# A graph network on one core: zero-fill copies cut into rows, and the matrix build in another order

## The chip, the cores and the metric

The kernel runs on one core of one Trainium2 chip. The metric is the device time of one execution in microseconds. Several executions were timed; one more was taken with the hardware profiler, and all rows shown below come from that one.

## What is computed

A graph of 1250 nodes, 512 features each, and 20000 edges sorted by target. Four layers follow each other, each added to its input and normalised:

```python
edge_index = jnp.stack([src, dst])
x = _layernorm(x + _L0_gnn_ref(x, edge_index, edge_weight, ...))      # weighted sum over edges
x = _layernorm(x + _L1_gnn_ref(x, edge_index, edge_type_2, ...))      # two relational layers, weights mixed from 30 bases
x = _layernorm(x + _L2_gnn_ref(x, edge_index, L2_gnn_W, L2_gnn_b))    # degree-normalised sum
x = _layernorm(x + _L3_gnn_ref(x, edge_index, edge_attr_8, ...))      # attention over edges with a bias for each edge
```

## The kernel before

Instead of gathering rows for each edge, the kernel turns the edge list into dense node-by-node matrices once and multiplies with them. Node counts are padded to 1280 (`NN`), ten tiles of 128 rows (`NT`). Five engines have programs of their own, written out by hand in the order in which they run; they meet only at semaphores.

**The build.** Edges lie in 160 chunks of 125. Because they are sorted by target, the edges of 32 target rows (a window) lie in a short range of chunks. There are 40 windows (`TT`), run as ten turns (`t4`) of four (`j`). For each window VectorE makes one-hot selections of the source node, 125 x 1250 in f16, one a chunk (lines 926 and 934), and TensorE multiplies each with the chunk's own values into three PSUM banks (line 1727, three matmuls a visit); windows alternate between two sets of three banks. Four visits (`FIXED`) are written out; the chunks beyond them, at least one a window, are visited in a loop over registers. The selections of the four lie in two sets of four buffers, those of the loop in a ring of `MORE` = 2. Each engine reads the chunk range of the next window from a table in SBUF into registers (`load_range`, lines 463 to 469). The order of a window before the change: on VectorE the first selection, the loop, the read of the range, selections two to four; on TensorE the first visit, the loop, one matmul of the second visit, the correction, the rest of the second visit, the third, the read of the range, the fourth.

ACT copies a finished window from PSUM to `stage16` in f16 (line 1398, `copied`). The correction `fix` on TensorE (line 1711) subtracts this f16 copy in the banks, so that what is left there is its error; ACT evicts that as the low half (line 1400, `evicted`), which frees the banks. SyncE stores the three parts of a window from `stage16` into the matrices `A16` and `CT` (lines 627 and 629, `R<-R`, three transfers of 80 KB); ACT waits for them (`stored`) before it writes the same of the four `stage16` slots again.

**The zero fill.** The attention's edge bias is a node-by-node table of 52 MB in DRAM (`bias_d`), which must be zero before GpSimd adds the edges into it by 160 indirect scatters (line 812). It is cut into 40 cells of 1.31 MB. The first is filled from SBUF; the others are DRAM-to-DRAM copies of it (line 779), all issued by GpSimd on the software queue: two at once, 24 during the build, one each time some windows are built (`built`), one after output tiles 8 and 9 of the first layer each (`o_done`), and eleven after the first relational layer's weights (`w_in`) and the edge data (`b_in`) have landed.

**After the build** come the ten output tiles of the first layer, with the mixing of the relational layer's weights between their matmuls. ACT and VectorE write the mixed weights out in two halves to DRAM (`w_d`, ACT's queue, 32 KB transfers, line 1351), and SyncE loads them back as `W<-w_d` (line 636) before TensorE's first z tile (line 1802), which waits for all four loads.

Of the kernel before, what the change touches and what calls it, by code (L numbers as in the profile page):

```python
# [6 lines left out]
F16 = mybir.dt.float16  # L7
# [8 lines left out]
NT = -(-NODES // P)  # L16
NN = NT * P
# [16 lines left out]
PIECES = [(0, 512), (512, 1024), (1024, NN)]  # L34
HOTS = 8
FIXED = 4
MORE = 2
BIG = 1e30
QUADS = 2
RB = 256  # L40
# [20 lines left out]
def gnn_resnorm(nc, a, out):  # L61
    ctx = ExitStack()
    with ctx:
# [47 lines left out]
        def in_w(n):  # L111
            nonlocal o
            o += n
            assert o <= 3 * FT * D
            return w_b[:, o - n:o]
# [3 lines left out]
        iota16 = in_w(NN // 2).bitcast(F16)  # L119
        tab = in_w(TT + 2)[0:1, :].bitcast(I32)  # L120
        fix16 = in_w(P // 2).bitcast(F16)
        zero = r3[:, NT * D + 2 * NN + CH:NT * D + 3 * NN + CH]
        more = zero.bitcast(F16).rearrange("p (s r) -> p s r", s=MORE)
        key = r3[:, NT * D + 2 * NN:NT * D + 2 * NN + CH]

        o = 0

        def tmp(n):
# [33 lines left out]
        lowrow = tmp(1)  # L162
        minus16 = tmp(P // 2).bitcast(F16)
        assert o <= 6 * NN // 2 + NN // 4
        o = NT * D + 3 * NN + CH
        SUPS = [[w_b[:, k * D // 2:(k + 1) * D // 2].bitcast(F16) for k in range(NT)],
                [w_b[:, (NT + k) * D // 2:(NT + k + 1) * D // 2].bitcast(F16) for k in range(6)] +
                [r3[:, o + k * D // 2:o + (k + 1) * D // 2].bitcast(F16) for k in range(4)]]
        assert o + 4 * D // 2 <= RELS * FT * NN
        wst_first = r1f[:, NT * NN // 2 - 4 * D:NT * NN // 2].bitcast(F16).rearrange(  # L170
            "p (g h q n) -> p g h q n", g=2, q=2, h=2)
        XTP = r3[:, 0:NT * D].rearrange("p (k f n) -> p k f n", k=NT, f=FT)
# [575 lines left out]
        def _(pool):  # L748
# [22 lines left out]
            def zeros(n):  # L771

                cells = bias_d[0:DUMP, :].rearrange("(n p s) h -> n p (s h)", n=ZF, p=P)
                if n < ZS:
                    pool.dma_start(cells[n].rearrange("p (a b) -> p a b", b=NN),
                                   zero.rearrange("p (u n) -> p u n", u=1).broadcast_to([P, 2, NN])).then_inc(
                                       zero_out, 16)
                else:
                    pool.dma_start(cells[n], cells[0]).then_inc(zero_out, 16)  # L779

            for i in range(2):
# [38 lines left out]
        def _(dve):  # L821
# [99 lines left out]
            def make(t4, j):  # L921

                lo, begin, end = range_of(dve, ranges[j % 2])

                def fixed(m):
                    V.tensor_scalar(hot[0:EC, FIXED * (j % 2) + m, 0:NODES], iota16[0:EC, 0:NODES], base[0:EC, bass.ds(t4, 1), j],  # L926
                                    key[0:EC, bass.ds(lo + m, 1)], ALU.add, ALU.is_equal).then_inc(hot_made, 1)

                dve.wait_ge(built, t4 * 4 + (j + 1))
                fixed(0)  # L930
                with dve.Fori(begin, end) as c:
                    v = dve.snap(visited, min_val=0, max_val=TT * CH)
                    dve.wait_ge(more_used, v + 1)
                    V.tensor_scalar(flat(more[0:EC, bass.ds(v & (MORE - 1), 1), 0:NODES]), iota16[0:EC, 0:NODES],
                                    base[0:EC, bass.ds(t4, 1), j], key[0:EC, bass.ds(c, 1)], ALU.add,
                                    ALU.is_equal).then_inc(more_made, 1)
                    dve.reg_add(visited, visited, 1)
                load_range(dve, ranges[(j + 1) % 2], t4 * 4 + (j + 1))
                for m in range(1, FIXED):
                    fixed(m)  # L940

            def windows(t4):
                for j in range(4):
# [11 lines left out]
            with dve.Fori(1, NT) as t4:  # L955
# [6 lines left out]
            V.tensor_copy(SUP[:, 1, 0:6, :].rearrange("p k f -> p (k f)"),  # L962
                          w_b[:, NT * D // 2:(NT + 6) * D // 2].bitcast(F16))
            V.tensor_copy(SUP[:, 1, 6:NT, :].rearrange("p k f -> p (k f)"),
                          r3[:, NT * D + 3 * NN + CH:NT * D + 3 * NN + CH + 4 * D // 2].bitcast(F16)).then_inc(sup_kept, 1)

            def turned_low(n, i):

# [354 lines left out]
        def _(act):  # L1323
# [84 lines left out]
            def mixed_high(m):  # L1408

                g, h = m // 2, m % 2  # L1410
                if h == 0 and m % MIXES >= 4:
                    act.wait_ge(w_stored, 64 * (g - 1))
                act.wait_ge(w_done, m + 1)
                S.activation(WST(m)[:, h, 0, :], mm_out(MIXED(m), D), ACT.Copy).then_inc(wh_made, 1)
                if h == 0 and m % MIXES and m != M0:
                    mix_stored(g - 1)
# [222 lines left out]
        def _(pe):  # L1639
# [80 lines left out]
            def build(j, t4, first):  # L1720
# [11 lines left out]
                def fixed(m, pieces=range(3)):  # L1732
                    if pieces[0] == 0:
                        pe.wait_ge(hot_made, t4 * 16 + (FIXED * j + m + 1))
                    return visit(lo + m, lambda p0, p1: hot[0:EC, FIXED * (j % 2) + m, p0:p1], m == 0, pieces)

                pe.wait_ge(evicted, t4 * 4 + (j + 1))
                fixed(0)
                with pe.Fori(begin, end) as c:
                    v = pe.snap(visited, min_val=0, max_val=TT * CH)  # L1740
                    pe.wait_ge(more_made, v + 1)
                    visit(c, lambda p0, p1: flat(more[0:EC, bass.ds(v & (MORE - 1), 1), p0:p1]),
                          False).then_inc(more_used, 1)
                    pe.reg_add(visited, visited, 1)
                fixed(1, range(1))
                if j:
                    fix(t4, j - 1)
                elif not first:
                    fix(t4 - 1, 3)
                fixed(1, range(1, 3))  # L1750
                fixed(2)
                load_range(pe, ranges[(j + 1) % 2], t4 * 4 + (j + 1))
                for m in range(3, FIXED):
                    ins = fixed(m)
                ins.then_inc(built, 1)

            pe.wait_ge(own_made, 1)
            pe.wait_ge(fix_made, 1)
# [473 lines left out]
```

## Time and profile before

| what | value |
|---|---|
| median of 3 runs | 1253.46 us |
| lowest and highest | 1247.01 and 1256.37 us |
| profiled execution | 1259.67 us |
| its span, first to last instruction | 1257.9 us |
| mean granted TensorE clock in it | 0.982 of full |

The profiled execution is 6.2 us longer than the median; 1.8 us of it lie around the span. Times in rows count from the span's start. Engines are PE (TensorE, PEld its weight loads), DVE (VectorE), ACT, POOL (GpSimd) and SP (SyncE); a q behind a name is the engine's sequencer or DMA queue. `R<-W,R` means that a tile R is written from tiles W and R.

### The profile page before, as it was taken

Reading aid. Unit: us, or ns where it says so; the run is one execution under the profiler, and the core shown is the slowest. Engines: PE = TensorE matmul, PEld = TensorE weight load, DVE = VectorE, ACT = ScalarE, POOL = GpSimd, SP = SyncE. Lnnn points to the kernel's source line nnn. Section 1 sums busy time; section 2 is a strip of 40 time slices with the busy share of each in tenths; the row PEclk is TensorE's granted clock in tenths of the full one; section 3 lists DMA queues with packets and bytes.
Section 4 is the critical chain, followed back from the end, with each engine's and each line's share of the span. In section 5 each row is a group of like instructions: output and inputs, shape, how many; then the busy total and the mean of one; then the engine's idle time right before and its main releaser. Section 6 shows DMA issues by size and latency. Waiting matters only on the chain.

```text
span 1257.9 us, 21464 instructions
## 1 busy us (share of the span) xinstructions
PE 1181.3 (94%) x8083; PEld 540.5 (43%) x8084; DVE 851.3 (68%) x1330; ACT 437.1 (35%) x586; POOL 307.6 (24%) x220
## 2 busy tenths in 40 slices
PE   6987879999999999999999999999999899999997
PEld 2333334323344334345445454455333365555553
DVE  7575657544434555553368875575999889899997
ACT  2444546512122222112311002216553255444454
POOL 2000000000010133344655655545556000000000
PEclk9988989999999999999999999999999899999999
DMA  8567867598799789753122213112223376565653
GB/s 327 209 217 247 297 224 269 151 407 305 243 363 307 257 285 314 278 165 109 2 35 35 50 19 69 2 3 33 34 33 67 139 235 231 202 220 187 213 186 112
DMA packets 64325, 222.73 MB, mean 177 GB/s; under 512 B 31138, under 2 KB 36002, under 8 KB 48272
## 3 DMA queue, kind: packets, MB, share of 16 engines
q1 hardware_dynamic: 34706, 156.38, 35.8%
q0 software_dynamic: 25184, 53.10, 16.7%
q10 hardware_dynamic: 4350, 12.07, 2.8%
q8 instruction: 60, 0.98, 0.3%
q14 instruction: 25, 0.20, 0.0%
HBM read 198.92 MB, written 59.92 MB: 206 GB/s over the span
## 4 chain that ended last, share of the span: by engine, by line
PE 69%; DVE 11%; issue 7%; DMA 7%; ACT 3%; SPq 2%; DVEq 1%; ACTq 0%
PE PS L1853 26%; PE PS L1802 10%; PE PS L1727 6%; PE PS L1657 5%; PE PS L2098 4%; PE PS L2085 4%; DMA R<-R 4%; DVE R L1172 4%; DVE R L1209 4%; PE PS L1675 3%; PE PS L1967 2%; PE PS L2144 2%; PE PS L1889 1%; PE PS L1773 1%; DMA W<-in_basis_s 1%
## 5 line engine op out<-in xcount | busy, mean ns | idle before, releaser
L812 POOL DMA_INDIRECT bias_d<-R x160 | 271.0, 1694 | 331.3 <-DMA bias_d<-R 220.5
L1853 PE MATMUL PS<-R 128*128 128x512 f16 x1300 | 298.1, 381 | 0.0
L1853 PEld LDWEIGHTS PS<-R 128*128 128x128 f16 x1300 | 120.5, 98 | 180.6 <-issue 49.7
L1727 PE MATMUL PS<-R,XX 125*128 125x512 f16 (+2 forms) x612 | 134.7, 354 | 15.3 <-ACT R L1400 6.8
L1613 ACT ACTIVATE R<-PS 128x1024 f32<-128x1024 f32 (+1 forms) x100 | 106.2, 1087 | 109.6 <-PE PS L2085 77.9
L1802 PE MATMUL PS<-W,XX 128*128 128x512 f16 x600 | 136.0, 386 | 5.1 <-DVE R L1010 2.7
L926 DVE TENSOR_SCALAR R<-W,R 125x1250 f16<-125x1250 f16 x160 | 89.4, 606 | 53.7 <-PE PS L1727 39.4
L1172 DVE CUSTOM_DVE_ANT_0 R<-PS,R 128x1250 f16<-128x1250 f32 x80 | 116.8, 1459 | 5.5 <-PE PS L2021 2.9
L2098 PE MATMUL PS<-R 128*32 128x256 f32 (+1 forms) x1600 | 102.5, 391 | 5.2 <-DVE R L1209 5.2
L2085 PE MATMUL PS<-R 128*128 128x256 f16 (+3 forms) x800 | 99.6, 275 | 5.4 <-ACT R L1613 2.2
L779 POOL DMA_DIRECT2D bias_d<-bias_d x39 | 21.6, 556 | 324.0 <-PE PS L1727 164.2
L1010 DVE SCALAR_TENSOR_TENSOR R<-PS,gate,R 128x512 f16<-128x512 f32 x50 | 37.4, 750 | 90.2 <-ACT R L1451 90.2
L1209 DVE SCALAR_TENSOR_TENSOR R<-R,W 128x512 f32<-128x512 f32 (+1 forms) x136 | 86.0, 673 | 15.9 <-ACT R L1613 14.1
L1727 PEld LDWEIGHTS PS<-R,XX 125*128 x612 | 58.3, 100 | 88.6 <-issue 57.5
L1802 PEld LDWEIGHTS PS<-W,XX 128*128 128x128 f16 x600 | 58.1, 99 | 76.9 <-issue 10.3
L2085 PEld LDWEIGHTS PS<-R 128*128 128x128 f16 (+1 forms) x800 | 74.7, 99 | 36.9 <-issue 20.6
L1434 ACT ACTIVATE stat<-stat 128x1 f32<-128x1 f32 x30 | 8.8, 294 | 184.1 <-DVE stat L998 171.7
L1451 ACT ACTIVATE R<-PS,gate 128x512 f16<-128x512 f32 x50 | 34.4, 687 | 98.1 <-PE PS L1802 97.4
L1400 ACT ACTIVATE R<-PS 32x1280 f32 x40 | 49.2, 1230 | 51.8 <-PE PS L1711 51.8
L2098 PEld LDWEIGHTS PS<-R 128*32 128x32 f32 x1600 | 44.8, 109 | 48.7 <-DVE R L1209 13.5
L1967 PE MATMUL PS<-XX,W 128*128 128x512 f16 (+1 forms) x288 | 61.3, 345 | 1.1 <-ACT R L1552 1.1
L970 DVE TENSOR_TENSOR XX<-PS,XX 128x512 f16<-128x512 f32 x40 | 27.5, 686 | 49.3 <-ACT XX L1405 46.7
(231 smaller groups left out, 1411.0 us busy)
## 6 DMA issues: line engine op xcount, KB each, us to landing
bias_d<-bias_d POOLq DMA_DIRECT2D x39, 1280.0 KB, 9.0
R<-in_basis_s SPq DMA_DIRECT2D x32, 1024.0 KB, 6.9
W<-in_basis_s SPq DMA_DIRECT2D x28, 1024.0 KB, 6.1
W<-bias_d SPq DMA_DIRECT2D x27, 1024.0 KB, 4.9
XX<-bias_d SPq DMA_DIRECT2D x13, 1024.0 KB, 4.9
R<-key_d SPq DMA_DIRECT2D x20, 500.0 KB, 4.0
R<-R SPq DMA_DIRECT2D x120, 80.0 KB, 5.9
W<-bias_d SPq DMA_DIRECT2D x7, 904.0 KB, 4.6
```

The costliest lines, as they stand in the source:

```text
L812: pool.indirect_dma_start(bias_d, bass.IndirectOffsetOnAxis(ap=idx[:, c:c + 1], axis=0), attr[:, c, :], None, bounds_check=DUMP + GC * P - ...
L926: V.tensor_scalar(hot[0:EC, FIXED * (j % 2) + m, 0:NODES], iota16[0:EC, 0:NODES], base[0:EC, bass.ds(t4, 1), j], key[0:EC, bass.ds(lo + m, ...
L1172: V.tensor_tensor_reduce(out=junk[:, 0:NODES], in0=PS[:, b0:b0 + 3, :].rearrange("p a b -> p (a b)")[:, 0:NODES], in1=nmask[:, i, 0:NODES] ...
L1209: ins = V.scalar_tensor_tensor(p, p, BIG, b, ALU.min, ALU.mult)
L1613: S.activation(ER[n % 4][:, :, 0:w, :].rearrange("p g r u -> p g u r"), PS[:, 2 * (n % 2):2 * (n % 2) + 2, :].rearrange("p a (e r) -> p a ...
L1657: ins = T.matmul(PS[32 * c:32 * c + RELS * FT, MIXED(m), :], attbd[0:BJ, layer, :, :].rearrange("p r j -> p (r j)"), BASIS(m)[0:BJ, c, :], ...
L1727: ins = T.matmul(mm_out(3 * (j % 2) + b, p1 - p0), own[0:EC, bass.ds(c, 1), :, :].rearrange("p c m w -> p (c m w)"), hots(p0, p1), start=f ...
L1802: ins = T.matmul(mm_out(zi % 2, D), lhs, rhs, start=n == 0, stop=n == len(terms) - 1)
L1853: ins = T.matmul(mm_out(SUM_BANK(s, i), D), lhs, rhs, start=n == 0, stop=n == len(terms) - 1)
L1967: ins = T.matmul(mm_out(BANK_OF("q", g), hi - lo), W16[:, 1 + which, q, f, o_ * P:(o_ + 1) * P], XT16[:, p, f, lo:hi], start=n == 0 and f ...
L2085: ins = T.matmul(PS[:, 2 * (n % 2) + i // 2, (i % 2) * RB:(i % 2) * RB + w], key[:, h, j * P:(j + 1) * P], query[:, h, cols], start=k == 0 ...
L2098: ins = T.matmul(PS[32 * i:32 * i + 32, 4 + q, e * RB:e * RB + w], VA[:, j, 4 * q + i, 32 * e:32 * e + 32], ER[n % 4][:, i // 2, 0:w, i % ...
```

## The change

Three things change together. The 39 copies of the zero fill take the 128 rows of 10 KB of a cell as even rows and then odd rows, on both sides, instead of as one piece. The order of a window changes: on VectorE three selections, the loop, the read of the range, the fourth selection; on TensorE two visits, the correction, the third visit, the loop, the read of the range, the fourth visit. And the loop's ring has four slots instead of two; to make room, `key` and four tiles of the first layer's support move to another tile (`W`), where the mixed weights will be staged, so ACT waits for `sup_kept` 2 before it writes the first of these.

```diff
-MORE = 2
+MORE = 4
...
-        zero = r3[:, NT * D + 2 * NN + CH:NT * D + 3 * NN + CH]
-        more = zero.bitcast(F16).rearrange("p (s r) -> p s r", s=MORE)
-        key = r3[:, NT * D + 2 * NN:NT * D + 2 * NN + CH]
+        key = in_w(CH)
+        sup_tail = in_w(4 * D // 2)
+        o = NT * D + 2 * NN
+        assert o + MORE * NN // 2 <= RELS * FT * NN
+        zero = r3[:, o:o + NN]
+        more = r3[:, o:o + MORE * NN // 2].bitcast(F16).rearrange("p (s r) -> p s r", s=MORE)
...
-                [r3[:, o + k * D // 2:o + (k + 1) * D // 2].bitcast(F16) for k in range(4)]]
+                [sup_tail[:, k * D // 2:(k + 1) * D // 2].bitcast(F16) for k in range(4)]]
...
-                    pool.dma_start(cells[n], cells[0]).then_inc(zero_out, 16)
+                    pool.dma_start(cells[n].rearrange("(a b) e -> b a e", b=2),
+                                   cells[0].rearrange("(a b) e -> b a e", b=2)).then_inc(zero_out, 16)
...
                 dve.wait_ge(built, t4 * 4 + (j + 1))
-                fixed(0)
+                for m in range(FIXED - 1):
+                    fixed(m)
                 with dve.Fori(begin, end) as c:
...
                 load_range(dve, ranges[(j + 1) % 2], t4 * 4 + (j + 1))
-                for m in range(1, FIXED):
-                    fixed(m)
+                fixed(FIXED - 1)
...
+                if m == M0:
+                    act.wait_ge(sup_kept, 2)
                 act.wait_ge(w_done, m + 1)
...
                 pe.wait_ge(evicted, t4 * 4 + (j + 1))
-                fixed(0)
+                for m in range(2):
+                    fixed(m)
+                if j:
+                    fix(t4, j - 1)
+                elif not first:
+                    fix(t4 - 1, 3)
+                for m in range(2, FIXED - 1):
+                    fixed(m)
                 with pe.Fori(begin, end) as c:
...
-                fixed(1, range(1))
-                if j:
-                    fix(t4, j - 1)
-                elif not first:
-                    fix(t4 - 1, 3)
-                fixed(1, range(1, 3))
-                fixed(2)
                 load_range(pe, ranges[(j + 1) % 2], t4 * 4 + (j + 1))
-                for m in range(3, FIXED):
-                    ins = fixed(m)
-                ins.then_inc(built, 1)
+                fixed(FIXED - 1).then_inc(built, 1)
```

## Rows read from the trace of the kernel before

**Rows 1.** Page, chain that ended last: share of the span by line.

```profile
PE PS L1853 26%; PE PS L1802 10%; PE PS L1727 6%; PE PS L1657 5%; PE PS L2098 4%; PE PS L2085 4%; DMA R<-R 4%; DVE R L1172 4%; DVE R L1209 4%; PE PS L1675 3%; PE PS L1967 2%; PE PS L2144 2%; PE PS L1889 1%; PE PS L1773 1%; DMA W<-in_basis_s 1%
```

**Rows 2.** Timeline of ACT, 217 to 246 us: start, duration, engine, line, operation.

```profile
219.26 1.24 ACT L1398 ACTIVATE R<-PS 128x1280 f16<-128x1280 f32 x1
...
242.11 1.24 ACT L1398 ACTIVATE R<-PS 128x1280 f16<-128x1280 f32 x1
```

**Rows 3.** Instructions of line 1398: durations, first and last start; idle before them until.

```profile
L1398 ACT ACTIVATE R<-PS x40: 1237/1237/1237, 72.2 to 242.1; 128x1280 f16<-128x1280 f32 x40
...
  DMA R<-R: 18.3, 6
```

**Rows 4.** Timeline of SyncE's issues, 204 to 222 us: start, duration.

```profile
205.34 3.69 SPq L627 DMA_DIRECT2D R<-R  x1
209.07 3.33 SPq L629 DMA_DIRECT2D R<-R  x2
...
219.96 1.23 SPq L629 DMA_DIRECT2D R<-R  x2
```

**Rows 5.** Chain that ended last, 207 to 213 us: start, duration, what.

```profile
208.00 1.24 PE PS L1727 x6
...
209.31 0.39 PE PS L1727
209.70 0.53 PE PS L1711 x3
210.23 1.37 PE PS L1727 x8
```

**Rows 6.** Chain that ended last, 120 to 126 us.

```profile
123.01 0.05 DVEq L931
...
123.95 0.09 DVE R L926
```

**Rows 7.** Instructions of line 465: ns min/median/max.

```profile
L465 PEldq TENSOR_LOAD <-W x41: 296/304/738, 63.8 to 240.1; - x41
```

**Rows 8.** DMA view: queues with packets, MB, share; issues with count, KB, landing.

```profile
q0 software_dynamic: 25184, 53.10, 16.7%
q10 hardware_dynamic: 4350, 12.07, 2.8%
...
bias_d<-bias_d POOLq DMA_DIRECT2D x39, 1280.0 KB, 9.0
...
w_d<-R ACTq DMA_DIRECT2D x80, 32.0 KB
...
w_d<-W ACTq DMA_DIRECT2D x48, 32.0 KB
...
R<-in_src_c SPq DMA_DIRECT2D x1, 78.1 KB, 3.3
key_d<-R SPq DMA_DIRECT2D x1, 78.1 KB, 19.8
R<-in_att_r ACTq DMA_DIRECT2D x2, 0.9 KB, 2.0
```

**Rows 9.** Windows: length, busy time of each engine, granted clock, DMA share, GB/s.

```profile
130.00:180.00 50.00, 38.72 (x192) 16.87 (x193) 31.03 (x56) 25.76 (x21) 4.88 (x8) 0.98 0.79 267
243.00:268.00 25.00, 21.55 (x112) 7.02 (x111) 8.37 (x17) 6.43 (x10) 0.00 (x0) 0.98 0.99 396
```

**Rows 10.** Chain that ended last, 330 to 360 us.

```profile
340.92 10.96 DMA W<-w_d
...
351.93 7.04 PE PS L1802 x24
```

**Rows 11.** Timeline of GpSimd, 340 to 440 us: idle before and its releaser in brackets.

```profile
340.46 0.49 POOL L779 DMA_DIRECT2D bias_d<-bias_d  x1 [7.14 <-PE PS L1853]
...
434.18 2.75 POOL L812 DMA_INDIRECT bias_d<-R  x1 [72.61 <-DVE R L1103]
```

**Rows 12.** Groups by line, 60 to 250 us: count, busy us, mean ns, idle.

```profile
L934 DVE TENSOR_SCALAR R<-W,R 125x1250 f16 x44 | 26.6, 604 | 5.1 <-PE PS L1727 5.1
```

More of the change, by code:

```diff
@@ L164, in gnn_resnorm @@
         assert o <= 6 * NN // 2 + NN // 4
-        o = NT * D + 3 * NN + CH
         SUPS = [[w_b[:, k * D // 2:(k + 1) * D // 2].bitcast(F16) for k in range(NT)],
                 [w_b[:, (NT + k) * D // 2:(NT + k + 1) * D // 2].bitcast(F16) for k in range(6)] +
-                [r3[:, o + k * D // 2:o + (k + 1) * D // 2].bitcast(F16) for k in range(4)]]
-        assert o + 4 * D // 2 <= RELS * FT * NN
+                [sup_tail[:, k * D // 2:(k + 1) * D // 2].bitcast(F16) for k in range(4)]]
         wst_first = r1f[:, NT * NN // 2 - 4 * D:NT * NN // 2].bitcast(F16).rearrange(
@@ L964, in _ @@
             V.tensor_copy(SUP[:, 1, 6:NT, :].rearrange("p k f -> p (k f)"),
-                          r3[:, NT * D + 3 * NN + CH:NT * D + 3 * NN + CH + 4 * D // 2].bitcast(F16)).then_inc(sup_kept, 1)
+                          sup_tail.bitcast(F16)).then_inc(sup_kept, 1)
             def turned_low(n, i):
```

## Prediction

> **What bounds the kernel now.** I read the chain of work that ended last first [rows 1]: its lines are mostly TensorE's, and the transfers with the largest share are the stores of the build, `R<-R`, 4%. The change touches the build (66 to 248 us) and the zero-fill copies, some of which fall behind the build, so I then looked at two places.
>
> The build makes 40 windows; ACT evicts each once at line 1398. In a quiet stretch seven of these evictions start between 219.26 and 242.11 us, six windows in 22.85 us: **3.81 us a window** [rows 2]. All 40 run from 72.25 to 242.11 us [rows 3], 39 steps in 169.86 us; at 3.81 they would take 148.6 us, so 21.3 us are lost somewhere. ACT's idle time before that line names most of it: 18.3 us, in six waits for `R<-R` [rows 3], the stores that must leave `stage16` before it is written again. The reader sees why in SyncE's issues: the three stores of a window cost about 0.6 us each when no copy runs, but 3.69 and 3.33 us, 7.0 us a window, beside one [rows 4]. A copy is cut today into 40 KB runs: of the software queue's 25184 packets [rows 8], 160 scatters (128 rows and 16 completions each) make 23040 and the first cell, 256 runs, 272; the other 1872 are 48 for each of 39 copies, 32 runs and 16 completions. Each store's 2.5 KB runs queue behind these.
>
> The quiet window itself [rows 5]: six matmuls (first selection and loop) 1.24, one matmul 0.39, the correction 0.53, eight matmuls 1.37; the last 0.3 of it is the loop's exit and a wait for ACT's eviction.
>
> **The copies' shape.** The new pattern has two as its outermost count, then 64 rows of 10 KB. The number of engines is the first unknown. What the trace shows: ACT's queue made 4350 packets [rows 8]. Its seven tile loads have 128 rows and, over 16 engines, 16 completions each: 1008. The two loads of 120 rows fit 15 completions: 270. The 128 stores of `w_d` are 32 KB in 2 KB runs over 8 partitions: 16 runs each. The 3072 packets that remain are 24 for each, so 8 completions: 8 engines, not 16. An outermost count of 8 got 8 engines, one of 120 got 15. So the ends are two engines (as that row has it for a small outermost count) and sixteen (as every copy of the software queue has now). I take **two**, the nearer row by shape. The Trainium skill (DMA: Bandwidth & Descriptors, "Why a DMA increments its semaphore by 16 and not by 1") states it as a rule: the engines are the largest number up to 16 that divides the slowest dimension, on the software queue too; the count above agrees for the hardware queue, and no row here shows it for the software one.
>
> How fast: 267 GB/s at a DMA share of 0.79 and 396 at 0.99 [rows 9] make 21.1 and 25.0 GB/s an engine. A copy of 1.31 MB on two engines then takes **26 to 31 us**, against a share of all sixteen now.
>
> How queues share an engine: `key_d<-R` is 78.1 KB in 500 B runs, ten an engine, and took 19.8 us beside the last eleven copies, where an equal load took 3.3 [rows 8]. Ten runs and a completion at 1.6 to 1.9 us, the length of one 40 KB run, is 18 to 21 us: one run of a copy for one run of the other queue. The Trainium skill (same page, "Queues, rings and completion order") has an engine drain a whole packet, some 9 to 17 runs, before it turns to another queue. By that, ten small runs would have gone through in one or two turns, and each store would sit behind 4 us or more of 10 KB runs. The row of `key_d` speaks against it.
>
> **Part 1, stores in the build.** With runs a quarter as long, the extra 5.2 us of SyncE's issues (7.0 less 1.8) become 1.3, so a window's stores take 3.1 us to issue, below the 3.81. This holds for two engines as for sixteen, since the slowest engine sets it. A part of the 21.3 us isn't stalls: the loop made 44 visits in 40 windows [rows 12], and four more at some 0.7 us (half of 1.24 and the exit) are 2.8. The rest, 18.5, agrees with ACT's 18.3: **−18**. Bounds: 0 (stores still late: on an engine in use the nine packets of a window, three stores of two runs and a completion, each wait for a 0.4 us run, together some 4 us) and −21.
>
> **Part 2, the order in the build.** Today the correction waits for nothing: from the window's start at 208.00 it is 1.70 us to the correction at 209.70 [rows 5], while ACT's copy of the window before (1.24 us [rows 2]) starts as that window ends. Behind two visits (1.04 us, from eight matmuls in 1.37) it arrives before the copy is done, so the cycle now closes through ACT: correction 0.53, third selection 0.52, the loop's entry, visit and exit 0.72 (half of 1.24, plus 0.1 for entry and exit), the read of the next range, last selection 0.52 and about 0.2 until its result is out, handover 0.04, ACT's copy 1.24, handover 0.04. Without the read that is 3.8, and 3.6 where the loop's entry and exit are covered too; 3.7 between them. The read now stands between the loop and the only matmuls that could cover it. On TensorE the table read alone takes 0.304 us [rows 7], with the register operations around it I count 0.4 to 0.5; on VectorE, where it stands behind the loop today, the path from the loop's end to the next operation is 123.01 to 123.95, 0.94 us [rows 6]. I take **4.2 us a window**: 39 × 0.4 = **+15.6**. Bounds: 3.6 (all covered: −8) and 4.5 (+28). VectorE's own window (5.1 selections of 0.60 us [rows 12] and the read) stays near 3.3 us and under this cycle. The ring of four takes away a wait of VectorE for the second loop visit, on the path only in windows with two visits: **−1** (0 to −4).
>
> ACT's new wait for `sup_kept` 2 stands ahead of its first mixed tile; queued behind it is only that tile and the norm that needs TensorE's first output tile later. Its cover is the landing of the basis tile that TensorE waits for; without that cover it costs under 1 us. `key` and the tail of the support in other places, and the longer descriptor writing of the copies on GpSimd, cost nothing: GpSimd idles for `built`.
>
> **Part 3, behind the build.** The 28th and 29th cells are filled after output tiles 8 and 9 of the first layer. The second of these copies is issued at 340.46 us, just as the four loads `W<-w_d` start at 340.92; they land 10.96 us later, and the first z tile starts at 351.93 [rows 10, 11]. All sixteen engines carry 131 KB of these weights each, in 128 runs of 1 KB. On the two engines that hold the second copy, its 64 runs alternate one for one with them, so all 64 pass before the weights are through: 342 + 26 + 5 (131 KB at 25 GB/s) = 373 instead of 351.9. TensorE has nothing else in its order: **+21**. Bounds: 0 (spread over sixteen engines: 8 runs of 0.4 us an engine, 3.3 us as 2 × 1.6 now), 27 (the 31 us copy). The last eleven copies follow the same wait; two on one pair take up to 62 us from 377, while the first scatter, 434.18 today [rows 11], moves to 455: covered to within some 15 us.
>
> **Sum.** −18 + 15.6 − 1 + 21 = +17.6. The profiled execution of 1259.67 us becomes 1277; it lies 6.2 us above the median of 1253.46, so on the median **1271**.
>
> **Rivals.**
> - *Copies on all sixteen engines, in 10 KB runs.* The weights land as today, the stores are relieved, and only the order pays: −18 + 15.6 − 1 = −3, **1250**. For it: every copy of that queue has sixteen engines now. Against: the shape, by [rows 8].
> - *The same, with the read of the ranges covered* (the other side). Its place is TensorE's queue behind the loop: where the last selection is queued in time, the cycle is 3.7 and the sum is −18 − 4 − 1 = −23, **1230**. It is faster by over 1% from a cycle of 3.97 us down. For it: today's read on TensorE isn't on the chain at all. Against: it has five matmuls queued ahead of it today and at most the loop's three then.
> - *The copies don't change:* the two views merge back into one contiguous stretch. Then the runs stay at 40 KB, stores stall as now where the slower cycle doesn't hide it: +15.6 less about half of 18, **1260**.
> - *Runs pass in blocks:* an engine that holds a copy lets many of its 64 runs through before a store's turn. Then the stalls of the build stay (0 for −18), **1289** or more. Against: `key_d` [rows 8]. This is what the packet of the Trainium skill (the section last named) would do here.
>
> **Chances.** Forecast 0.60 (in it, some 0.10 where a covered read or a shorter hold brings it within 1%); sixteen engines 0.17; sixteen and covered 0.12; unchanged copies 0.08; blocks 0.03. One per cent, 12.5 us, is about what a measurement of this kernel tells from no change. Faster 0.12; within 1%: 0.10 + 0.17 + 0.05 = 0.32; slower 0.56. The range takes in the two middle cases and the dearer read: **1246 to 1288**; the faster case lies outside.
>
> **What would show it.** Right: a copy's median landing of 25 to 35 us (9.0 now); no wait of ACT line 1398 for `R<-R`; eviction starts 4.2 us apart; TensorE waiting some 20 us for `W<-w_d` near 350 us. Wrong: copies that land in under 12 us (sixteen engines); a cadence at or below 3.8 (the read is covered); `R<-R` waits that stay (the store's place in the queue isn't set by the length of one run).

## The result, and the profile after

The changed kernel takes **1308.88 us** (median of 4 runs, 1303.79 to 1312.03) against 1250.24 us of the kernel before in the same session (4 runs, 1243.11 to 1256.37): ratio 1.0452, 95% interval 1.0403 to 1.0501. It is slower by 58.6 us; the prediction was 1271 with a range to 1288, so the sign was right and the time lies outside.

The profiled execution of the changed kernel took 1303.79 us (span 1302.0), the one of before 1259.67 (span 1257.9): the two traces differ by 44.1 us. Before's profiled execution lies above its median and this one is the lowest of its four, so a trace accounts for 44 of the 58.6 us; the medians of the experiments below account for the whole.

The page of the changed kernel, queues and DMA issues, against [rows 8]:

```profile
q0 software_dynamic: 63872, 53.24, 16.7%
...
bias_d<-bias_d POOLq DMA_DIRECT2D x39, 1280.0 KB, 18.2
```

Take the 23040 packets of the scatters and the 272 of the first cell off, as in the prediction, and 40560 are left for 39 copies: **1040 each**.
```profile
DMA to landing us min/median/max: 3.4/18.2/89.6
```

1.31 MB in 3.4 us would be 193 GB/s an engine. In the trace's records of single DMA packets a 10 KB row takes 0.385 us (median), which is 26.6 GB/s, so the 64 rows of an engine take **24.6 us**. Between 384 and 400 us the two copies issued at 379.00 (below) are all that GpSimd has out, on four engines, and the window agrees (length, busy time of each engine, granted clock, DMA share, GB/s): 113 GB/s is 28 an engine, if all of it is theirs.

```profile
384.00:400.00 16.00, 16.00 (x87) 7.44 (x85) 4.71 (x7) 4.10 (x8) 0.00 (x0) 1.00 0.28 113
```

The evictions of the build, instructions of line 1400 (line 1398 before), against [rows 3], with ACT's idle time before them:

```profile
L1400 ACT ACTIVATE R<-PS x40: 1237/1237/1239, 73.6 to 245.2; 128x1280 f16<-128x1280 f32 x40
...
  PE PS L1731: 48.6, 40
```

The waits for `R<-R` (18.3 us in six) are gone; all 40 evictions now wait for TensorE. But 39 steps take 171.6 us, 1.7 more than before. One window of the chain that ended last (start, duration, what) says why, against [rows 5]:

```profile
219.68 1.25 ACT R L1400
220.93 0.05 issue
220.98 0.70 PE PS L1715 x3
221.68 1.06 PE PS L1731 x6
222.74 0.47 issue
223.21 0.71 PE PS L1731 x3
...
223.95 1.25 ACT R L1400
```

The cycle closes through ACT as forecast: copy, correction (line 1715), third selection and loop, 0.47 us in which TensorE's sequencer reads the next range, last selection, next copy. It is 4.27 us long; 3.81 before.

Behind the build, GpSimd's timeline (start, duration, instruction, in brackets the idle time before it and what ended it), against [rows 11]:

```profile
144.15 0.89 POOL L780 DMA_DIRECT2D bias_d<-bias_d  x1 [7.59 <-PE PS L1731]
176.57 5.27 POOL L780 DMA_DIRECT2D bias_d<-bias_d  x6 [31.53 <-issue]
...
379.00 1.57 POOL L780 DMA_DIRECT2D bias_d<-bias_d  x2 [34.22 <-DMA R<-in_attr_t]
408.24 7.13 POOL L780 DMA_DIRECT2D bias_d<-bias_d  x9 [27.66 <-issue]
...
505.05 1.69 POOL L814 DMA_INDIRECT bias_d<-R  x1 [89.30 <-DMA bias_d<-bias_d]
```

The row at 144.15 is the 15th copy. Then GpSimd stands still for 31.5 us with nothing to wait for but its own issue, and writes six copies in a row. The same happens behind the 30th copy, for 27.7 us. In the packet records the last of what it had issued ends at 175.66 and at 407.41, so it goes on 0.8 to 0.9 us after all of it has been moved. Hence the last nine are issued at 408 and the first scatter starts at 505.05 instead of 434.18, waiting for the zero fill.

The chain that ended last behind the build, against [rows 10]:

```profile
345.13 30.56 DMA W<-w_d
375.74 7.11 PE PS L1804 x24
...
433.86 18.48 DMA W<-in_basis_s
...
477.73 26.60 DMA R<-in_basis_s
...
619.29 5.34 PE PS L1804 x24
...
1041.69 3.57 PE PS L2087 x16
```

The weights take 30.56 us instead of 10.96, and the first z tile starts 23.8 us late (375.74 for 351.93; 3.1 of it is the build's later end). The packet records show the hold itself: from 351 to 357 us there are 56 runs of 10 KB in GpSimd's queue and 56 of 1 KB in SyncE's, one for one, and the last 10 KB run ends at 375.06. Two loads of basis tiles stand bare on the chain; in the chain of before, the same z phase of the next layer starts at 583.08, so the delay is now 36.2. From there to the score phase (997.40 before) the chain runs over scatters, and the delay is 44.3, which is the delay of the end. TensorE's idle time by groups shows the waits (count, busy, mean | idle and what ended it):

```profile
L2087 PE MATMUL PS<-R 128*128 128x256 f16 (+3 forms) x800 | 100.9, 277 | 13.1 <-DMA R<-R 9.8 <-ACT R L1617 2.2 <-DVE R L1174 1.1
...
L1661 PE MATMUL PS<-R,attbd 120*8 120x512 f32 x288 | 38.0, 599 | 6.2 <-DMA R<-in_basis_s 4.2 <-ACT R L1376 1.4 <-DVE W L980 0.6
...
L1661 PE MATMUL PS<-W,attbd 120*8 120x512 f32 x224 | 29.8, 603 | 9.4 <-DMA W<-in_basis_s 9.3
```

So in the traces: build +3, hold of the weights +21 (with 1.1 us between the build and the loads), basis loads +12, scatters +8.

### The profile page after: what moved, and what is told of

Its sections match the earlier page's. It is cut to its first block, busy times and chain, and to the rows that moved or that the text cites. A ratio compares the mean times of both kernels' runs of the same rounds, so it can differ in the third digit from the quotient of the medians.

```text
span 1302.0 us, 21464 instructions
## 1 busy us (share of the span) xinstructions
PE 1178.9 (91%) x8083; PEld 538.2 (41%) x8084; DVE 851.6 (65%) x1330; ACT 437.4 (34%) x586; POOL 314.1 (24%) x220
## 2 busy tenths in 40 slices
DMA packets 103014, 222.87 MB, mean 171 GB/s; under 512 B 66083, under 2 KB 70947, under 8 KB 83217
## 4 chain that ended last, share of the span: by engine, by line
PE 52%; DMA 21%; issue 9%; DVE 7%; POOL 5%; ACT 4%; DVEq 1%; ACTq 1%; SPq 0%; POOLq 0%
PE PS L1855 17%; DMA bias_d<-R 10%; PE PS L1804 7%; PE PS L1731 6%; POOL bias_d L814 5%; PE PS L2100 5%; PE PS L2087 4%; PE PS L1661 4%; DVE R L1211 3%; DMA W<-w_d 2%; ACT R L1400 2%; DMA W<-in_basis_s 2%; DMA R<-in_basis_s 2%; PE PS L1715 2%; PE PS L2146 2%
## 5 line engine op out<-in xcount | busy, mean ns | idle before, releaser
L814 POOL DMA_INDIRECT bias_d<-R x160 | 266.0, 1663 | 341.9 <-DMA bias_d<-R 213.7
L1804 PE MATMUL PS<-W,XX 128*128 128x512 f16 x600 | 134.4, 383 | 25.4 <-DMA W<-w_d 22.0
L1731 PE MATMUL PS<-R,XX 125*128 125x512 f16 (+2 forms) x612 | 124.7, 343 | 25.9 <-issue 16.4
L928 DVE TENSOR_SCALAR R<-W 125x1250 f16<-125x1250 f16 x160 | 92.8, 624 | 58.4 <-PE PS L1731 54.9
L780 POOL DMA_DIRECT2D bias_d<-bias_d x39 | 33.1, 852 | 366.7 <-PE PS L1855 136.2
L1400 ACT ACTIVATE R<-PS 128x1280 f16<-128x1280 f32 x40 | 49.5, 1237 | 48.6 <-PE PS L1731 48.6
## 6 DMA issues: line engine op xcount, KB each, us to landing
bias_d<-bias_d POOLq DMA_DIRECT2D x39, 1280.0 KB, 18.2
```

Of the source, the lines that this page charges most:

```text
L814: pool.indirect_dma_start(bias_d, bass.IndirectOffsetOnAxis(ap=idx[:, c:c + 1], axis=0), attr[:, c, :], None, bounds_check=DUMP + GC * P - ...
L1400: S.activation(stage16[:, j, :], banks[:, 0:NN], ACT.Copy).then_inc(copied, 1)
L1731: ins = T.matmul(mm_out(3 * (j % 2) + b, p1 - p0), own[0:EC, bass.ds(c, 1), :, :].rearrange("p c m w -> p (c m w)"), hots(p0, p1), start=f ...
L1804: ins = T.matmul(mm_out(zi % 2, D), lhs, rhs, start=n == 0, stop=n == len(terms) - 1)
```

## The experiments

All are the kernel before or the changed kernel with a few lines edited. "Sixteen engines" below is this form of a copy, the first half's rows interleaved with the second's, which has 64 as its outermost count and also runs of 10 KB:

```diff
-pool.dma_start(cells[n].rearrange("(a b) e -> b a e", b=2),
-               cells[0].rearrange("(a b) e -> b a e", b=2))
+pool.dma_start(cells[n].rearrange("(b a) e -> a b e", b=2),
+               cells[0].rearrange("(b a) e -> a b e", b=2))
```

| kernel | median us | ratio to before | weights' load | first scatter |
|---|---|---|---|---|
| rows_only | 1294.65 | 1.0354 [1.0304, 1.0405] | 30.93 | 500.56 |
| order_only | 1261.24 | 1.0092 [1.0059, 1.0125] | 11.65 | 438.77 |
| half_rows_only | 1240.61 | 0.9928 [0.9903, 0.9953] | 10.65 | 418.63 |
| order_half_rows | 1257.02 | 1.0044 [1.0012, 1.0077] | 11.93 | 435.38 |
| two_in_build | 1261.20 | 1.0073 [1.0041, 1.0105] | 11.03 | 442.61 |
| two_but_weights | 1262.88 | 1.0092 [1.0044, 1.0141] | 10.70 | 451.55 |
| two_but_last | 1281.79 | 1.0242 [1.0186, 1.0298] | 31.04 | 458.12 |
| four_engines | 1266.69 | 1.0122 [1.0075, 1.0169] | 21.28 | 445.96 |
| two_behind_build | 1301.18 | 1.0416 [1.0346, 1.0486] | not on it | 505.07 |
| no_second_stop | 1283.52 | 1.0251 [1.0197, 1.0305] | 30.81 | 463.71 |
| early_read | 1261.17 | 1.0063 [1.0030, 1.0096] | 10.47 | 432.61 |
| early_read_ring2 | 1257.45 | 1.0039 [1.0008, 1.0071] | 10.65 | 432.18 |
| read_then_fix | 1239.74 | 0.9879 [0.9815, 0.9943] | 10.89 | 414.49 |
| late_fix | 1245.76 | 0.9994 [0.9962, 1.0026] | 10.62 | 420.56 |
| read_before_fix | 1232.94 | 0.9881 [0.9807, 0.9955] | 12.05 | 411.20 |

(The weights' load is `DMA W<-w_d` in the chain that ended last, the first scatter is from GpSimd's timeline, both in us.)

### Which part is it: shape or order

**rows_only**, the kernel before with the changed copies alone.

```diff
-pool.dma_start(cells[n], cells[0])
+pool.dma_start(cells[n].rearrange("(a b) e -> b a e", b=2),
+               cells[0].rearrange("(a b) e -> b a e", b=2))
```

> The kernel before with the copies in even and odd rows alone. Theory A (the copies' two engines cost the time: the weights' load waits 21 us, and GpSimd, held up in issuing, pushes the last copies into the next layer's loads and the scatters, some 20 us more; the build's stalls of 18 us go): +21 +20 -18, 20 to 35 us slower than before, about 1280 us; W<-w_d takes about 30 us to land, GpSimd has one or two idle stretches of about 30 us in front of a copy, evictions of the build 3.8 us apart. Rival B (the order of the window costs it): the stalls go and nothing else, about 1232 us.

**order_only**, the changed kernel with the copies of before (the reverse of that edit).

> The changed kernel with the copies in one piece again, so the order of a window, the ring of four and the moved tiles alone. Theory A: 4.24 us a window instead of 3.81, 16 us, and about 1 us more in each of five windows with two visits, from which the stalls hide a part, as the stores have more time: 5 to 15 us slower than before, about 1260 us; W<-w_d lands in 11 us as before and GpSimd doesn't stand still in issuing. Rival B: nearly all of the loss, 40 us or more, about 1300 us.

**half_rows_only**, the kernel before with sixteen-engine copies, and **order_half_rows**, the changed kernel with them.

> The kernel before with the copies as 10 KB rows over sixteen engines (outermost count 64) alone. Theory A: the build's stalls go and its cadence stays 3.81 us: 18 us faster, about 1232 us. Rival C: slower than before. A third way: the stores are held by nine small runs an engine for each copy as long as by two large ones, then no change, 1250 us.

> The changed kernel with the same 10 KB rows taken in another order: 64 outermost, two inside (a row of the upper half, then one of the lower), so that the outermost count is 64. Theory A: sixteen engines, a copy lands in about 9 us or less beside other work, no stall of the stores, no hold of the weights beyond the 11 us of before, no standstill of GpSimd; only the order is left: -18 +16 +5, about 1253 us. Rival C (10 KB runs as such cost it, by four times as many packets): as slow as the changed kernel, about 1300 us.

The shape of the copies alone costs 3.5%, dearer than theory A had it; the order alone costs 0.9%. Copies in 10 KB runs on sixteen engines, which no part of the change is, make the kernel before 0.7% faster; the interval lies below 1, though half of theory A's 18 us is missing. In half_rows_only, line 1399 and the first z tile of the chain show where:

```profile
L1399 ACT ACTIVATE R<-PS x40: 1237/1237/1237, 72.1 to 224.7; 128x1280 f16<-128x1280 f32 x40
```

```profile
334.87 8.31 PE PS L1803 x24
```

39 steps take 152.6 us, 17.3 less than before, and z starts 17.1 us sooner than 351.93: the stalls of the stores came from the length of the copies' runs. The profiled spans differ by 15.0 us, the medians by 9; the profiled execution of before lies above its median, and whether an ordinary execution of it loses less to stalls wasn't traced. Between half_rows_only and order_half_rows there is only the order: **+16.4 us**.

rows_only doesn't gain in z what it gains in the build (its evictions end at 230.3): the chain shows eight waits for stores `w_d<-W` between 260 and 340 us, 4.7 to 7.4 us each, and then the weights' 30.93.

### Which copies: in the build, at the weights, or the last

In the changed kernel, `b` in the pattern `"(a b) e -> b a e"` is 2 for every copy; here it is 64 (sixteen engines) for some.

```diff
+b = 2 if n < ZE + ZB else P // 2                    # two_in_build
+b = 2 if not ZE + ZB <= n < ZE + ZB + 2 else P // 2 # two_but_weights
+b = 2 if n < ZE + ZB + 2 else P // 2                # two_but_last
```

> The changed kernel, but the thirteen copies behind the build go out in a shape that uses all sixteen engines; the copies of the build stay on two. Theory A (the loss has three parts, all behind the build: the weights' loads queue behind two-engine copies, about 21 us; GpSimd stands still with its queue full and the late copies fall on the basis loads, about 12 us; the late scatters, about 8 us): all three go, the first load of W from w_d takes 11 to 13 us instead of 30.6, the median is 1255 to 1268. Rival B (the two-visit order of the build costs most): 1300 or more. Rival C (two-engine copies harm wherever they lie, in the build as much as behind it): 1280 to 1295.

> The changed kernel, but only the two copies that are issued just ahead of the weights' loads use sixteen engines. Theory A (hold of the weights and late copies are separate terms): the load of W from w_d takes 11 to 16 us, the basis loads are still late by 9 to 13 us and the scatters by 8, so 1280 to 1292. Rival D (everything late follows from the hold of the weights alone): 1255 to 1268. Rival E (copies issued earlier still stand in the two engines' queues when the loads come, so that the hold stays): 1300 or more.

> The changed kernel, but the last eleven copies use sixteen engines. Theory A: the hold of the weights stays (the load of W from w_d at 28 to 32 us), GpSimd doesn't stand still a second time, or not for 25 us, the basis loads and scatters are on time: 1280 to 1292. Rival D (what is late follows from the hold of the weights): 1300 to 1312. Rival F (the late copies are the larger part): 1265 to 1278.

two_in_build goes as theory A has it: with the thirteen copies behind the build on sixteen engines, 47.7 of the 58.6 us are gone, and two engines up to the build's end cost 4.2 (against order_half_rows; the two intervals overlap). In the traces this cost lies ahead of the build, not in it: the evictions of two_in_build start later but take no longer (170.9 us for 39 steps, 170.5 in order_half_rows, second line).

```profile
L1401 ACT ACTIVATE R<-PS x40: 1237/1237/1239, 78.4 to 249.3; 128x1280 f16<-128x1280 f32 x40
L1400 ACT ACTIVATE R<-PS x40: 1237/1237/1238, 71.9 to 242.4; 128x1280 f16<-128x1280 f32 x40
```

The other two say that theory A's terms don't add: the hold alone (two_but_last) costs 20.6 us over two_in_build, the last copies alone (two_but_weights) 1.7, which is within the noise, both together 47.7. two_but_last lies in theory A's range, two_but_weights came out as rival D had it, though GpSimd stands still there just the same, in its timeline:

```profile
391.00 5.48 POOL L781 DMA_DIRECT2D bias_d<-bias_d  x7 [30.18 <-issue]
...
451.55 1.69 POOL L815 DMA_INDIRECT bias_d<-R  x1 [54.69 <-DMA bias_d<-bias_d]
```

while two_but_last, with the hold and no second standstill, has all eleven copies out at once and its scatters at 458.12:

```profile
378.94 6.37 POOL L781 DMA_DIRECT2D bias_d<-bias_d  x11 [34.50 <-DMA R<-in_attr_t]
```

### Why GpSimd stands still

**four_engines**: `b=4` for every copy of the changed kernel, 32 rows on each of four engines.

> The changed kernel with every copy as four sets of 32 rows of 10 KB instead of two sets of 64. Theory A with queue places (a copy takes as many places in all sixteen queues as the longest set has rows, so 33 instead of 65, and GpSimd stands still when about a thousand are taken): no standstill of 30 us behind the 15th copy, one at most near the 30th; a copy lands in about 10 us instead of 18; the packets of GpSimd's queue stay near 64000 (128 rows and 12 x 32 + 16 small ones a copy, 528 x 39, would be 43900 in all); the load of W takes 17 to 22 us; 1262 to 1280. Rival G (GpSimd stands still by the number of copies, not by places): the same standstill behind the 15th copy, and 1285 to 1305.

Its queue row, the weights in its chain, and GpSimd's timeline:

```profile
q0 software_dynamic: 43904, 53.16, 16.3%
```

```profile
342.39 21.28 DMA W<-w_d
```

```profile
386.04 6.17 POOL L780 DMA_DIRECT2D bias_d<-bias_d  x9 [17.70 <-issue]
```

43904 is exactly 23312 + 39 x 528, with 528 = 128 rows + 12 idle engines x 32 + 16 completions; the "near 64000" of the expectation contradicts the sum beside it, and the sum was right. The standstill behind the 15th copy is gone; one comes behind the 30th. So it goes by places in the queue: 33 a copy here (528 / 16), 65 in the change, 9 with sixteen engines (144 / 16). The hold is halved with the rows that an engine has: 32 rows at 0.385 us are 12.3 us. (The 10 us expected for a copy, and the 13.8 of the page, are landings, which don't measure it.)

**two_behind_build** and **no_second_stop** were to settle where the 25 us come from that the hold and the last copies make only together: the standstill between them, or the shape of the last copies.

```diff
+b = P // 2 if n < ZE + ZB else 2        # two_behind_build
+b = P // 2 if 16 < n < ZE + ZB else 2   # no_second_stop
```

> The changed kernel, but the 26 copies of the build use sixteen engines; the thirteen behind it stay on two, so that the weights are held and the last eleven copies are two-engine copies as in the change, but thirteen such copies (13 x 65 = 845 places) don't fill GpSimd's queue. Theory A' (the loss beyond the hold comes from GpSimd's second standstill: it keeps the last nine copies back for 28 us, in which the DMA engines are busy for 0.29 only, and so pushes them onto the basis loads and the scatters): no standstill, the last copies are issued in one go near 380, the DMA share between 380 and 408 us is over 0.6, the first scatter starts before 485, and the median is 1275 to 1290. Rival K (the last copies' two-engine shape itself collides with the basis loads once the hold has moved it, standstill or not): 1298 to 1310.

The median came out as rival K had it, but the run didn't do what it was made for. GpSimd's timeline:

```profile
372.77 7.03 POOL L781 DMA_DIRECT2D bias_d<-bias_d  x9 [34.10 <-DMA R<-in_attr_t]
443.51 1.67 POOL L781 DMA_DIRECT2D bias_d<-bias_d  x2 [63.70 <-issue]
```

It stands still for 63.7 us ahead of the last two copies, though the first 28 had all been moved by 369.16 in the packet records. Counting the places from the start, drained or not, explains this row and all others: 17 for the first cell (272 / 16), 26 x 9 and 11 x 65 are 966, and the next copy would make 1031. In the change, 17 + 15 x 65 = 992, the next 1057; behind the first standstill 15 x 65 = 975 again, the next 1040. In four_engines 17 + 30 x 33 = 1007 still went, 1040 didn't. So a standstill comes when the places taken since the last one would pass a number between 1007 and 1031, even where most of those transfers are long done, and it ends when all are.

> The changed kernel, but the 17th to 26th copy use sixteen engines. In two_behind_build GpSimd stood still after all, behind the 37th copy: places count up from the start, drained or not (17 for the first cell, 26 x 9 and 11 x 65 make 966, the next would be 1031), and it goes on when its transfers are done. Here the first standstill stays at the 16th copy, and behind it 65 + 10 x 9 + 13 x 65 = 1000 places follow, as many as four_engines took without one (17 + 30 x 33 = 1007): so no second standstill, all last eleven copies issued in one go near 380. Theory A' (the second standstill makes the 25 us beyond the hold): 1275 to 1290, the first scatter before 485. Rival K (the last eleven on two engines collide with the basis loads whenever the hold has moved them): 1296 to 1310, the first scatter near 500.

GpSimd's timeline, and windows of 380 to 408 us (length, busy time of each engine, granted clock, DMA share, GB/s) of no_second_stop, then of the changed kernel:

```profile
378.90 8.62 POOL L781 DMA_DIRECT2D bias_d<-bias_d  x11 [34.72 <-DMA R<-in_attr_t]
...
463.71 1.69 POOL L815 DMA_INDIRECT bias_d<-R  x1 [75.82 <-DMA bias_d<-bias_d]
```

```profile
380.00:408.00 28.00, 28.00 (x154) 13.34 (x153) 9.54 (x17) 7.83 (x13) 7.89 (x11) 1.00 1.03 328
```

```profile
380.00:408.00 28.00, 28.00 (x155) 13.31 (x153) 9.59 (x18) 8.11 (x13) 0.58 (x1) 1.00 0.29 105
```

The hold and the thirteen two-engine copies behind the build are there, the second standstill is gone: 1283.52, **25.4 us less than the change**. The ten copies of the build that use sixteen engines here don't explain it, for the first z tile starts when it did in the change (375.74):

```profile
375.75 7.45 PE PS L1805 x24
```

From there the trace is 19.7 us shorter, the 12 of the basis loads and the 8 of the scatters. And the median is 1.7 us from two_but_last's, where the last eleven use sixteen engines, so their shape alone costs nothing that these runs can tell; rival K is out. While GpSimd stands still, the DMA engines are busy for 0.29, and what could have been written then falls on the basis loads and ahead of the scatters. Without the hold (two_but_weights) the standstill ends at 391 instead of 408, with seven copies behind it instead of nine, and nearly nothing waits for it; which of these two differences makes it harmless wasn't separated.

### Which part of the order

**early_read**: order_half_rows with TensorE's read ahead of the loop; **early_read_ring2** the same with `MORE = 2`; **read_then_fix** also has the correction behind three visits.

```diff
 for m in range(2, FIXED - 1):
     fixed(m)
+load_range(pe, ranges[(j + 1) % 2], t4 * 4 + (j + 1))
 with pe.Fori(begin, end) as c:
     ...
-load_range(pe, ranges[(j + 1) % 2], t4 * 4 + (j + 1))
 fixed(FIXED - 1).then_inc(built, 1)
```

> The changed kernel with zero-fill copies in 10 KB runs over sixteen engines, and TensorE's read of the next range ahead of the loop instead of behind it. Theory A (the new order costs 0.4 us a window because that read stands between the loop and the last selection, on the cycle through ScalarE's copy): the evictions come 3.75 to 3.85 us apart instead of 4.24, 39 x 0.44 = 17 us less than the same kernel with the late read: 1237 to 1244. Rival H (the correction's wait for ScalarE's copy sets the cycle, wherever the read stands): 4.1 to 4.25 us, 1252 to 1260.

> As early_read, with a ring of two selections for the loop as in the kernel before. The prediction put the ring at -1 us (0 to -4): this is 0 to 4 us slower than early_read. Rival: VectorE makes the loop's selections too late with two, more than 6 us slower.

> As early_read, with the correction behind three visits instead of two (three visits, read, correction, loop, last visit). Theory A: the cycle through ScalarE is then copy 1.25 + correction 0.70 + loop 0.5 + last visit 0.7 + handovers 0.1 = 3.25 us, less than TensorE's own matmuls (3.5), so TensorE becomes the bound: 3.5 to 3.75 us a window and 1232 to 1241. Rival: the third visit was hidden already, the cadence stays as in early_read, within 3 us of it.

Moving the read alone gained nothing, against theory A: the time is a microsecond above rival H's range. A window of early_read, chain that ended last:

```profile
217.26 1.25 ACT R L1400
...
218.56 0.70 PE PS L1715 x3
219.26 0.53 PE PS L1731 x3
219.79 0.23 issue
220.02 0.69 PE PS L1731 x3
...
220.76 0.71 PE PS L1731 x3
```

The cycle is still 4.24 us: the 0.47 of the read has split into 0.23 ahead of the loop and matmuls that no longer overlap (0.53 + 0.69 for 1.06). The ring of two was no slower (1257.45 for 1261.17, intervals that overlap). read_then_fix was faster by 21 us and lies in theory A's range, but not by theory A's cycle: the middle one of its 39 steps is 3.88 us, not 3.5 to 3.75, and TensorE isn't the bound. The chain goes through ACT's second eviction (line 1402), which frees the banks:

```profile
179.18 1.24 ACT R L1402
180.42 0.22 issue
180.64 1.76 PE PS L1731 x9
```

It also moved two things. So two more, each of which moves one, from order_half_rows:

```diff
 for m in range(2):
     fixed(m)
+load_range(pe, ranges[(j + 1) % 2], t4 * 4 + (j + 1))   # read_before_fix; deleted behind the loop
+fixed(2)                                                # late_fix; deleted behind fix
...
 fix(t4, j - 1)
...
```

> As order_half_rows (copies in 10 KB runs on sixteen engines, the changed order), with TensorE's read of the next range ahead of the correction, so that it falls into the time in which TensorE waits for ScalarE's copy. Theory I (TensorE's instructions pass in order: the correction's wait for the copy holds back the read and the loop's register work too, and early_read gained nothing because the read still stood behind that wait): the cycle is copy 1.25 + 0.05 + correction 0.70 + third and loop's visits 1.06 + 0.1 + last visit 0.70 = 3.86 us, 15 us less in 39 steps, 1240 to 1248. Rival J (the read isn't on the cycle at all; the correction behind ScalarE's copy alone makes the 4.24): 4.15 to 4.25 us, 1253 to 1261.

> As order_half_rows, with the correction behind three visits instead of two and the read left behind the loop. By theory I the copy (1.25 us) is over before the correction is reached (three visits, some 1.6 to 1.8 us), so nothing waits for it, and the read still stands bare between the loop and the last visit: 1.76 + 0.54 + 0.5 + 0.45 + 0.70 = 3.95 us, with bounds 3.85 and 4.1, 1243 to 1252. By rival J, for which the correction's place is all: 3.85 to 3.9 us as in read_then_fix, 1237 to 1243.

read_before_fix, line 1400 and one window of its chain:

```profile
L1400 ACT ACTIVATE R<-PS x40: 1237/1237/1237, 71.3 to 217.8; 128x1280 f16<-128x1280 f32 x40
```

```profile
196.01 1.25 ACT R L1400
197.26 0.05 issue
197.30 0.70 PE PS L1715 x3
198.00 1.60 PE PS L1731 x9
...
199.63 1.25 ACT R L1400
```

3.62 us a window, and rival J is out. Theory I has the place right and its 3.86 was too long, so that the time lies 7 us under its range: third, loop's and last visit now run as nine matmuls in 1.60. The place of the read makes the difference: it must stand ahead of the correction's wait for ACT's copy (3.62 us), not merely ahead of the loop (4.24 in early_read, where it was queued behind that wait). These two runs fit a sequencer that takes its instructions in order, as theory I has it. late_fix, with the correction moved and the read left bare, lies inside theory I's bounds (the middle one of its 39 steps is 3.98 us; all of them, with the windows of two visits, make 4.11 on average) and not at rival J's.

read_before_fix with sixteen-engine copies is the fastest of these versions by its median: 1232.94 us, ratio 0.9881 [0.9807, 0.9955] to before, 76 us under the change. read_then_fix has the same ratio, and half_rows_only is under the kernel before, too.

## Why the prediction was wrong, by its steps

| term, us | predicted | measured, by medians |
|---|---|---|
| 10 KB runs, stalls of the stores | -18 | -9 (half_rows_only); -17.3 in the trace of the build |
| order of the window | +15.6 - 1 | +16.4 (order_half_rows less half_rows_only) |
| two engines up to the build's end | 0 | +4.2 (two_in_build less order_half_rows) |
| weights' hold | +21 | +20.6 (two_but_last less two_in_build) |
| last copies, without the hold | 0 | +1.7 (two_but_weights less two_in_build) |
| GpSimd's second standstill behind the hold | 0 | +25.4 (the change less no_second_stop) |
| sum | +17.6 | +59.3 (measured: +58.6) |

Each measured term is a difference of two medians. Those of +4.2 and +25.4 come from two sessions each, between which the medians of before differ by 1 to 2 us; +4.2 and +1.7 are within the noise.

- **The step that failed** is in Part 2 and Part 3: "the longer descriptor writing of the copies on GpSimd, cost nothing: GpSimd idles for `built`", and the last eleven copies "covered to within some 15 us". Both took GpSimd as free to issue whenever its semaphores allow. A copy on two engines takes 65 places in the queue of every engine, and GpSimd stood still twice. Nothing in the trace of before showed it: at 48 packets a copy, 3 on each engine, there was room. The cover of the last copies was worked out from their transfer alone. With nine of them issued at 408 instead of 379, the loss fell first on the basis loads (12 us in the traces), which use the same engines and which the prediction didn't name, and then on the scatters (8). The transfer was reckoned too short as well: with no second standstill (no_second_stop) the copies issued from 378.90 on hold the first scatter to 463.71, 85 us for "up to 62", but that costs next to nothing.
- **Two engines** was right: what [rows 8] show for a hardware queue holds for the software one, by 1040 packets a copy. The Trainium skill (DMA: Bandwidth & Descriptors, "Why a DMA increments its semaphore by 16 and not by 1") gives the same rule for both, the largest number up to 16 that divides the slowest dimension. These packets, with 528 a copy at an outermost count of four, agree.
- **The hold of the weights** was right in mechanism and size. A copy's rows take 24.6 us by the packet records where 26 to 31 was worked out from [rows 9], runs of the two queues pass one for one (56 and 56 from 351 to 357 us), and the first z tile starts at 375.74 where 373 was reckoned. The sign chosen for it, a median landing of 25 to 35 us, failed (18.2), because that row doesn't measure a copy's transfer.
- **The stalls of the stores** went as forecast, and with them the rival of runs that pass in blocks: no wait for `R<-R` is left. In medians the gain is half as large; that difference is open.
- **The order** was right in size and place (4.2 forecast, 4.27 measured), and in the change the read wasn't covered, as the forecast took it. The rival with a covered read came close with 1230 against 1232.94 for read_before_fix, in part by luck: the 10 KB runs gave -9 where it has -18, and the cycle 3.62 where it has 3.7.
- **The ring** is worth nothing that these runs can tell.
- Two bounds are off in their own sums: 39 windows at 4.5 us are +27, not +28, and the hold behind a 31 us copy is 26, not 27. Nothing hangs on them.

## What to carry to other kernels

Before a DMA's pattern is changed, count on how many engines its outermost count puts it and how many queue places it takes on all of them; then ask not only who waits for the transfer but whether the issuing engine can still issue. Costs on one chain of covers need not add: a hold of 21 us and late copies that were worth 2 us without it made 48 together, so run the pair as well as each alone. Look at a landing's smallest value before its median is taken for a transfer's time. And a register read for a sequencer belongs ahead of the first instruction that waits for another engine, not merely ahead of the one that needs it (0.62 of 4.24 us a window here).

## What the runs showed of the hardware that was not expected

- A software-queue copy on k of 16 engines puts as many small packets on each idle engine as the longest used one has rows: 1040 packets a copy with two engines, 528 with four, 144 with sixteen.
- GpSimd stands still in its issue once the places taken since the last standstill would pass a number between 1007 and 1031, even if most of those before are drained: 31.5 us behind the 15th copy, 27.7 behind the 30th, 63.7 in two_behind_build. It goes on about 1 us after the last of its packets (175.66, 407.41 and 442.41).
- A 10 KB row inside HBM took 0.385 us (median) on its engine, with two engines to a copy as with four and with sixteen: 26.6 GB/s an engine, 24.6 us for the 64 rows of a copy on two.
